# Graph layer on one core: the third expert layer in products of 512 columns, its tiles issued in two parts

## The reference, cut to what matters

```python
xn = layernorm(x)                                   # [3125, 256]
w = softmax(xn @ Wr + br)                           # [3125, 8], one gate per node and expert
h = relu(bn(einsum('fd,edh->feh', xn, W1) + b1))    # first layer
h = relu(bn(einsum('feh,ehk->fek', h, W2) + b2))    # second layer
y = einsum('feh,ehd->fed', h, Wo) + bo              # third layer
out = x + einsum('fed,fe->fd', y, w)                # gated sum over the experts
```

## Time and profile before

| what | value |
|---|---|
| three executions | 1117.34, 1115.76, 1119.72 us; median 1117.34 |
| profiled execution | 1118.59 us, its span 1116.6 us |
| PE busy | 945.6 us (85%), 5218 products |
| DVE busy | 749.9 us (67%), 1412 instructions |
| ACT busy | 586.4 us (53%) |
| third layer L1023 to L1025, products of 256 columns | 3 x 200 rows, 283 ns each |
| addition of outputs L1689 | 200 rows, 476 ns each |

### The profile page before, as it was taken

One profiled execution on the slowest core, in us unless ns is written; L12 is line 12 of the kernel. 1 busy time (PEld: TensorE's weight loads), 2 busy tenths in 40 slices (PEclk: granted clock), 3 DMA queues, 4 the chain that ended last, 5 costly groups with the idle time before them and its releaser, 6 DMA issues.

```text
span 1116.6 us, 15043 instructions
## 1 busy us (share of the span) xinstructions
PE 945.6 (85%) x5218; PEld 822.9 (74%) x5218; DVE 749.9 (67%) x1412; ACT 586.4 (53%) x1206; POOL 380.2 (34%) x408
## 2 busy tenths in 40 slices
PE   6868588887885889788863569999999999999997
PEld 5656477666774778666753458899998989898987
DVE  6748578767865787778785777787555655555554
ACT  4720155454553456364542336667756566666664
POOL 0236566666666666666667600000000000000000
PEclk9879799989987898888987769999999999999999
DMA  8414344344444344344436410020000000000012
GB/s 252 141 53 113 102 125 118 101 127 113 116 116 109 97 125 117 102 126 111 119 103 200 116 47 15 15 69 1 29 1 30 1 29 1 29 1 1 1 32 84
DMA packets 50362, 89.02 MB, mean 80 GB/s; under 512 B 9732, under 2 KB 33336, under 8 KB 50267
## 3 DMA queue, kind: packets, MB, share of 16 engines
q0 software_dynamic: 18768, 52.88, 17.5%
q1 hardware_dynamic: 30780, 34.66, 10.0%
q10 hardware_dynamic: 719, 0.27, 0.1%
HBM read 81.10 MB, written 6.68 MB: 79 GB/s over the span
## 4 chain that ended last, share of the span: by engine, by line
PE 51%; another core or an unknown queue 16%; ACT 15%; DVE 11%; issue 6%; DMA 0%; DVEq 0%; ACTq 0%
PE bank L1023 11%; PE bank L1025 11%; PE bank L1024 11%; PE bank L942 4%; PE bank L896 4%; ACT junk L579 2%; PE bank L817 2%; PE bank L852 2%; PE bank L949 1%; PE bank L931 1%; DVE oh L1360 1%; PE bank L810 1%; ACT TT L598 1%; ACT U L588 1%
## 5 line engine op out<-in xcount | busy, mean ns | idle before, releaser
L472 POOL DMA_INDIRECT G<-projected_rows,src_l x391 | 377.5, 965 | 260.9 <-issue 109.1
L721 ACT ACTIVATE hid<-bank,faff 128x512 f32<-128x512 f32 (+2 forms) x224 | 157.7, 723 | 115.5 <-PE bank L1025 113.7
L896 PE MATMUL bank<-G,oh 128*128 128x264 f32 x782 | 190.1, 402 | 18.9 <-DVE G L1383 10.8
L896 PEld LDWEIGHTS bank<-G,oh 128*128 128x128 f32 x782 | 154.7, 199 | 47.1 <-DVE G L1383 10.9
L1677 DVE TENSOR_TENSOR hil<-hid,hil 128x1024 fp32r<-128x1024 f32 (+2 forms) x56 | 61.0, 1089 | 101.2 <-ACT hil L729 101.2
L1383 DVE TENSOR_TENSOR G<-G,bank 128x3072 f32<-128x3072 f32 (+1 forms) x33 | 109.1, 3307 | 0.0
L604 ACT COPY feat_rows<-bank 128x256 f32<-128x256 f32 x25 | 9.3, 373 | 171.9 <-remote 163.1
L931 PE MATMUL bank<-feat_rows,wqkv 128*128 128x256 f32 (+1 forms) x312 | 75.3, 382 | 17.6 <-DVE baff L1484 11.4
L1023 PE MATMUL bank<-frh,ew 128*128 128x512 f32 (+3 forms) x228 | 84.9, 372 | 3.8 <-DVE frl L1652 3.8
L1689 DVE SCALAR_TENSOR_TENSOR feat_rows<-bank,gate,feat_rows 128x256 f32<-128x256 f32 (+1 forms) x200 | 83.2, 476 | 4.3 <-PE bank L1025 4.3
L1024 PE MATMUL bank<-frl,ew 128*128 128x512 f32 (+3 forms) x228 | 82.9, 364 | 0.0
(11 more groups left out here) (326 smaller groups left out, 2105.4 us busy)
## 6 DMA issues: line engine op xcount, KB each, us to landing
dstb<-targets SPq DMA_DIRECT2D x32, 384.0 KB, 5.1
G<-projected_rows,src_l POOLq DMA_INDIRECT x391
projected_rows<-sums SPq DMA_DIRECT2D x25, 132.0 KB, 2.2
x_in<-in_x SPq DMA_DIRECT2D x3, 1024.0 KB, 9.3
out<-feat_rows SPq DMA_DIRECT2D x23, 128.0 KB, 2.2
U<-in_x SPq DMA_DIRECT2D x4, 512.0 KB
TT<-in_W SPq DMA_DIRECT2D x8, 256.0 KB
wqkv<-in_W SPq DMA_DIRECT2D x8, 256.0 KB
```

The costliest lines, as they stand in the source:

```text
L472: g.indirect_dma_start(out=G[slot][:, c, :], out_offset=None, in_=table[:, :], in_offset=bass.IndirectOffsetOnAxis(ap=src_l[:, grp, c:c + ...
L721: A.activation(hid[layer][:, m, 0:cols], bank[2 * layer + m][:, 0:cols], ACT.Relu, bias=faff[:, 2 * layer + 1, j:j + 1], scale=faff[:, 2 * ...
L896: ins = T.matmul(b_seg[g % 2][:, 0:ROW], oh[g % 2][:, c, :], G[g % SLOTS][:, c, :], start=(c == 0), stop=(c == ch - 1))
```

## The change

The third layer's product of the high hidden values with both parts of the weights becomes one product of 512 columns (high weights and low weights side by side), in both halves k; the low hidden values by the high weights stay products of 256 columns. So a tile takes four products instead of six, and fills a whole bank with two sums of 256 columns. DVE adds both to `mixed`, with a wait between them. Every tile is a piece of its own: `third` signals `y_mm` per tile, `add_outputs` waits and signals per tile.

Since a tile takes a bank, the order changes. In steps below `WIDE` = 23, while banks 6 and 7 are in use, only banks 4 and 5 serve. PE issues tiles 0 and 1 behind the second layer of the next step, and tiles 2 and 3 (or 2) behind the first layer after that; DVE likewise. From step 23 on tile i has bank 4 + i, and all tiles are issued in one go. The shares are taken in seven groups of up to four tiles (`QUADS`), two tiles per bank, so that `WIDE` can begin at step 23, and DVE adds two tiles with one operation.

```diff
-PAIRS = [range(t, min(t + 2, NT)) for t in range(0, NT, 2)]
+QUADS = [[[t for t in (start + q, start + 4 + q) if t < NT] for q in range(2)]
+         for octet in range(0, NT, 8) for start in (octet, octet + 2) if start < NT]
...
+WIDE = SHARE + len(QUADS) + 1
...
+def pieces(n):
+    tiles = list(range(BLOCK_TILES[STEPS[n][1]]))
+    return [tiles[i:i + 1] for i in range(len(tiles))] if n >= 0 else [tiles[i:i + 2] for i in range(0, len(tiles), 2)]
+
+PIECES_TO = [0]
+for step in range(len(STEPS)):
+    PIECES_TO.append(PIECES_TO[-1] + len(pieces(step)))
...
-        def outputs_of(b):
-
-            for j in range(-(-columns(b) // P)):
-                size = min(P, columns(b) - j * P)
-                yield j, slice(j * P, j * P + size), bank[4 + j // 2][0:size, (j % 2) * F:(j % 2 + 1) * F]
+        def output_of(n, i, j):
+
+            size = min(P, columns(STEPS[n][1]) - j * P)
+            y = bank[4 + (i if n >= WIDE else i % 2)][0:size, 0:2 * F]
+            return slice(j * P, j * P + size), y
...
-            def third(n):
+            def third(n, chosen):
...
-                need(pe, s["y_add"], n)
-                for j, nodes_, y in outputs_of(b):
-                    for k in range(KC):
-                        ins = split_product(y, hidh[1][par][:, k, nodes_], hidl[1][par][:, k, nodes_], ew[:, e % 2, 0, 2, k, :], ew[:, e % 2, 1, 2, k, :], k)
-                ins.then_inc(s["y_mm"], 1)
+                if n == WIDE:
+                    pe.wait_ge(s["x2b"], SHARE_SUMS[-1])
+                for i in chosen:
+                    tiles = pieces(n)[i]
+                    if n < WIDE:
+                        need(pe, s["y_add"], PIECES_TO[n] + max(i - 1, 0))
+                    else:
+                        need(pe, s["y_add"], PIECES_TO[n - 1] + (min(i + 1, len(pieces(n - 1))) if n > WIDE else len(pieces(n - 1))))
+                    for j in tiles:
+                        nodes_, y = output_of(n, i, j)
+                        w = ew[:, e % 2, :, 2, :, :]
+                        lh, ll = hidh[1][par], hidl[1][par]
+                        high = y.rearrange("p (q f) -> p q f", q=2)
+                        T.matmul(high, lh[:, 0, nodes_], w[:, :, 0, :], start=True, stop=False)
+                        T.matmul(y[:, 0:F], ll[:, 0, nodes_], w[:, 0, 0, :], start=False, stop=False)
+                        T.matmul(y[:, 0:F], ll[:, 1, nodes_], w[:, 0, 1, :], start=False, stop=False)
+                        ins = T.matmul(high, lh[:, 1, nodes_], w[:, :, 1, :], start=False, stop=True)
+                    ins.then_inc(s["y_mm"], 1)
...
+                if 2 <= n < WIDE + 2 and len(pieces(n - 2)) > 2:
+                    third(n - 2, range(2, len(pieces(n - 2))))
                 second(n)
...
-                    third(n - 1)
+                    third(n - 1, range(2) if n - 1 < WIDE else range(len(pieces(n - 1))))
...
-            def add_outputs(n):
+            def add_outputs(n, chosen):
...
-                dve.wait_ge(s["y_mm"], n + 1)
-                need(dve, s["y_add"], n)
-                for j, nodes_, y in outputs_of(b):
...
+                need(dve, s["y_add"], PIECES_TO[n] + chosen[0] if len(chosen) else 0)
+                for i in chosen:
+                    tiles = pieces(n)[i]
+                    dve.wait_ge(s["y_mm"], PIECES_TO[n] + i + 1)
+                    for j in tiles:
...
+                        high, low_ = (y[:, q * F:(q + 1) * F].rearrange("p (c n) -> p c n", c=KC) for q in range(2))
+                        link(V.scalar_tensor_tensor(out=m, in0=high, scalar=gate[0:rows, t, e:e + 1], in1=m, op0=ALU.mult, op1=ALU.add))
+                        ins = V.scalar_tensor_tensor(out=m, in0=low_, scalar=gate[0:rows, t, e:e + 1], in1=m, op0=ALU.mult, op1=ALU.add)
+                    ins.then_inc(s["y_tile"] if n == len(STEPS) - 1 else s["y_add"], 1)
...
+            def add_shares(i, added):
+                quad = QUADS[i - 1]
+                dve.wait_ge(s["y_add"], added)
+                dve.wait_ge(s["bo_mm"], SHARE_TILES[i])
+                for q, tiles in enumerate(quad):
+                    m = mixed[:, tiles[0]:tiles[-1] + 1:STRIPS]
+                    V.tensor_tensor(m, m, bank[6 + q][:, 0:len(tiles) * F].rearrange("p (t c n) -> p t c n", c=KC, n=P), ALU.add).then_inc(s["x2b"], 1)
...
+                if 2 <= n < WIDE + 2 and len(pieces(n - 2)) > 2:
+                    add_outputs(n - 2, range(2, len(pieces(n - 2))))
                 if odd and b + 2 < BLOCKS:
                     statistics(b + 3)
...
-                    add_outputs(n - 1)
+                    add_outputs(n - 1, range(2) if n - 1 < WIDE else range(len(pieces(n - 1))))
```

More of the change, by code:

```diff
@@ L1 @@
+import itertools
 import math
@@ L78 @@
 NA = 16
-PAIRS = [range(t, min(t + 2, NT)) for t in range(0, NT, 2)]
+QUADS = [[[t for t in (start + q, start + 4 + q) if t < NT] for q in range(2)]
+         for octet in range(0, NT, 8) for start in (octet, octet + 2) if start < NT]
+QUADS = [[tiles for tiles in quad if tiles] for quad in QUADS]
+SHARE_SUMS, SHARE_TILES = [0], [0]
+for quad in QUADS:
+    SHARE_SUMS.append(SHARE_SUMS[-1] + len(quad))
+    SHARE_TILES.append(SHARE_TILES[-1] + sum(map(len, quad)))
+WIDE = SHARE + len(QUADS) + 1
 PIECES = HALVES[0] + list(zip(FIRST_TILE[1:], BLOCK_TILES[1:]))
@@ L432, in _ @@
             for b in range(BLOCKS - 1):
-                sp.wait_ge(s["y_add"], full + b + 1)
+                sp.wait_ge(s["y_add"], PIECES_TO[full + b + 1])
                 for t in tiles_of(b):
@@ L615, in split_weights @@
             def split_weights(e, m):
-                ends = ("h1_mm", KC), ("h2_mm", KC), ("y_mm", 1)
                 act.wait_ge(w_raw[e % 2], 48 * (e // 2 + 1))
@@ L620, in split_weights @@
                 else:
-                    act.wait_ge(s[ends[m][0]], ends[m][1] * (LAST_STEP[e - 2] + 1))
+                    done = LAST_STEP[e - 2] + 1
+                    signal, count = (("h1_mm", KC * done), ("h2_mm", KC * done), ("y_mm", PIECES_TO[done]))[m]
+                    act.wait_ge(s[signal], count)
                 A.copy(ew[:, e % 2, 0, m], raw[e % 2][:, m]).then_inc(s["w_hi"], 1)
@@ L726, in hidden @@
                 else:
-                    need(act, s["y_mm"], n - 1)
+                    need(act, s["y_mm"], PIECES_TO[max(n - 1, 0)])
                 act.wait_ge(done, n * KC + KC)
@@ L1088, in shares @@
                     pe.wait_ge(s["gt_ready"], 1)
-                for t in PAIRS[i - 1]:
-                    need(pe, s["x2b"], t - 1)
+                need(pe, s["x2b"], SHARE_SUMS[i - 1])
+                for part, q in itertools.product(range(2), range(2)):
+                    tiles = (QUADS[i - 1] + [[]])[q]
+                    if part >= len(tiles):
+                        continue
+                    t = tiles[part]
                     row = t % STRIPS * STRIP
-                    T.matmul(bank[6 + t % 2][:, 0:F], gT3[row:row + STRIP, t // STRIPS * P:(t // STRIPS + 1) * P],
+                    T.matmul(bank[6 + q][:, part * F:(part + 1) * F], gT3[row:row + STRIP, t // STRIPS * P:(t // STRIPS + 1) * P],
                              bo_split[row:row + STRIP, :], start=True, stop=True).then_inc(s["bo_mm"], 1)
@@ L1114, in _ @@
                 if n >= 1:
-                    third(n - 1)
+                    third(n - 1, range(2) if n - 1 < WIDE else range(len(pieces(n - 1))))
                 if n == SHARE:
                     gates_turned()
-                if SHARE < n <= SHARE + len(PAIRS):
+                if SHARE < n <= SHARE + len(QUADS):
                     shares(n - SHARE)
-            third(total - 1)
+            third(total - 1, range(len(pieces(total - 1))))
         @block.vector
@@ L1701, in split_gates @@
                 V.scalar_tensor_tensor(out=bo_split, in0=bo_raw, scalar=low[:, 0:1], in1=bo_hi, op0=ALU.mult, op1=ALU.add).then_inc(s["g3_in"], 1)
[L1703 to L1708 removed]
+            def add_shares(i, added):
[5 more added lines that the diff above has]
+                    V.tensor_tensor(m, m, bank[6 + q][:, 0:len(tiles) * F].rearrange("p (t c n) -> p t c n", c=KC, n=P), ALU.add).then_inc(s["x2b"], 1)
+                dve.wait_ge(s["x2b"], SHARE_SUMS[i])
             def rest_rows_of(b):
@@ L1759, in _ @@
                     split_gates()
-                if SHARE < n <= SHARE + len(PAIRS):
-                    add_shares(n - SHARE)
-            add_outputs(total - 1)
+                if SHARE < n <= SHARE + len(QUADS):
+                    add_shares(n - SHARE, PIECES_TO[n - 1] + 2)
+            add_outputs(total - 1, range(len(pieces(total - 1))))
 def _layout(i):
```

19 lines of the change are left out of this document (4 added, 15 removed).

## The result

The change makes the kernel slower: 1159.24 us median of four (1155.99 to 1160.63) against 1118.22 of four of the kernel before, a ratio of 1.0374 with an interval of 1.0358 to 1.0389. That is 41.0 us more; forecast were 37.2 more, 1154.5, in a range of 1141 to 1168.

What follows compares the result with a forecast made beforehand. PE was taken to bound the kernel, so any PE wait for DVE is lost in full. Terms 6.4 + 4.7 + 13.9 + 1.4 + 13.7 - 1.6 - 2.7 + 0.4 + 1 = +37.2 on 1117.3 gave 1154.5 us, range 1141 to 1168.

Steps and rivals of the forecast that it cites:

- The wide products: Third layer: a tile takes 0.691 us instead of 0.708, 0.017 less; -2.7 us over 156 tiles from step 12 on.
- The stalls of steps 13 to 24: PE waits for adds queued behind remainders on in-order DVE, 5.31 us against 4.11 of PE work; twelve stalls, +13.7 us.
- The interleaved steps: Steps 2 to 10: DVE's extra adds lengthen the loop; +4.7 us from R2 to R4, +13.9 from R4 to R10.
- R2: Start of step 2's second remainder (R(n) likewise for step n); forecast 709.6 instead of 703.19, +6.4 us.
- The clock: Start: new PE gaps, between 2.6 and 8.1 us, may lower the clock; charged +1 us, bounds 0 and 10.
- of which DVE's loop hides part: Start: a low clock for 5 us costs about 2.5 of PE time, partly hidden by DVE's loop; +1 us taken.
- The small edits: Shares of the output bias in 7 groups instead of 13, -1.6 us; the last two steps' adds, +0.4.
- B: Rival: only DVE's throughput counts, its idle time takes most of the extra work; about 1120 us, chance 0.04.
- D: Rival: the late steps wait too, 32 steps at 1 us more; about 1187 us, chance 0.03.
- E: Rival: faster, the stall in steps 13 to 24 vanishes as the second add costs nothing; about 1113 us, chance 0.03.
- C: Rival: the clock drops in the gaps of several steps, 5 us a stretch; about 1167 us, chance 0.07.
- F: Rival: the product with the two-piece operand is slow; +3 us, inside the forecast, no chance of its own.

Runs made afterwards that it cites:

- e1: The change, but DVE adds tiles 2 and 3 of a step ahead of the next first layer's remainder: 1147.21 us, ratio 1.0234 to the kernel before.
- e4: As e3, but in steps 0 to 22 tiles 2 and 3 are placed as in the change, still one add a tile: 1129.92 us, ratio 1.0075.
- e5: Kernel before in steps 0 to 13, the change's new order in 14 to 22, wide from 23, seven share groups: 1122.67 us against 1115.47.
- e2: The change, but in steps 0 to 22 DVE adds only each tile's high half, one operation: 1139.79 us, ratio 1.0171 to the kernel before.
- e7: The change with useless products in the start's two long PE gaps (20 and 16 of 512 columns): 1153.22 us against 1115.47 before.
- e6: The kernel before in all steps, with only the shares in seven groups of four tiles: 1113.96 us against 1115.47, ratio 0.9983.
- e3: Steps 0 to 22 as in the kernel before, 23 to 55 wide and shares as in the change: 1116.68 us against 1121.40, ratio 0.9960.
- e8: The change, but tiles 0 and 1 of a narrow step wait only for their own bank's add: 1152.27 us against 1115.47, ratio 1.0328.
- e9: The change with the edits of e1 and e8 together, on another chip: 1050.36 us against 1022.66 for the kernel before, ratio 1.0248.

## Why the prediction was right, point by point

**What bounds the kernel** was read rightly. PE had no slack, so its waits for DVE showed in the time, and the late steps stayed bound by PE: DVE's 76 us of work per 100 in them did not matter.

**The wide products** gave what the rows said. In step 48 four products make a tile, and tiles begin 0.70 us apart:

```profile
1043.92 0.40 PE L1105 MATMUL bank<-ew,even 128*128 128x512 f32 x1
1044.15 0.28 PE L1106 MATMUL bank<-ew,even 128*128 128x256 f32 x1
1044.27 0.28 PE L1107 MATMUL bank<-ew,even 128*128 128x256 f32 x1
1044.39 0.40 PE L1108 MATMUL bank<-ew,even 128*128 128x512 f32 x1
1044.62 0.40 PE L1105 MATMUL bank<-ew,even 128*128 128x512 f32 x1
```

From R30 to R53 the changed kernel gains 1.5 us on the one before over 83 tiles, 0.018 a tile, where the sum has 0.017. The two-piece operand costs nothing that can be seen. The estimate by the Trainium skill's fixed part (TensorE: Matmul & The Clock Gate, Back-to-back issue gap), a third of that, was too low here; the measurement decides.

**The stalls of steps 13 to 24.** The stage grew by 14.6 us, and e1, which takes only the order away, gives back 10.9 of them. The pattern was right as well: forecast were stalls of 2.0, 1.0, 1.0, 1.2, 0.6, 1.25, 0.9, 2.0, 1.0, 1.0 and 1.2, and the steps R14 to R24 are longer by 2.2, 1.4, 1.0, 1.3, 0.9, 1.2, 1.2, 2.2, 1.5, 1.1 and 0.8. The step that says why, "tile 0 for *all* adds of the step before", "behind the remainder", is shown by e1, e4 and e5, and its size by e5. They are undersized by 2.2 us: up to R24 the sum has eleven stalls, 13.2, less 0.7 for the wide products. About 0.9 of that is in the restarts: a product behind a wait has a row of 0.47 instead of 0.40, and the next one starts 0.31 behind it (857.94 and 858.25) instead of 0.23. Where the other 1.3 lies is open.

**The interleaved steps** came out at 5.4 and 13.6 for 4.7 and 13.9. Here the chain was right turn by turn, and not only in total: behind R4 the three periods were put at 23.6, 22.3 and 20.8 and are 23.5, 22.1 and 20.8. Of the 19.0 us that R2 to R10 grows, 8.3 go with the second addition (e2: 83.5 us instead of 91.8; before 72.8), 3.5 come between e4 (80.0) and e2, and 7.2 with the placement, part of it a low clock behind e4's gap.

**The clock** is the term that was mis-sized: it was charged with 1 and cost 2.5. "The new gaps lie between" was the open point. Gaps of 4.7 and 6.4 us did bring it down to its lower level (1.2 GHz), twice for some 7 us (a mean of 0.66 over 10 us is 6.8 us at half, 0.76 and 0.90 are 4.8 and 2.0 us). The first products behind them last 0.77 instead of 0.47 us:

```profile
694.25 0.77 PE L1105 MATMUL bank<-ew,even 128*128 128x512 f32 x1 [4.72 <-DVE feat_rows L1733]
...
707.85 0.76 PE L1105 MATMUL bank<-ew,odd 128*128 128x512 f32 x1 [6.44 <-DVE feat_rows L1733]
```

The step that failed is "of which DVE's loop hides part". In the time of this execution, 2.6 us earlier, the sum's chain has A(0) tile 2 at 694.3, which is what the row shows, the end of S(2) at 698.6 and R2 at 707.0. S(2) ended at 700.4 and R2 came at 708.81: 1.8 us late at both, so nothing was hidden. The second spell cost 0.6 more. DVE had to wait for PE's scores, which the chain of the sum doesn't have, and tile 0 of the next third layer, its tile 2 and R4 are each 0.6 to 0.7 later than R2 and the sum's distances give:

```profile
715.98 0.23 DVE L1698 TENSOR_REDUCE gate<-bank 128x32 f32<-128x64 f32 x1 [0.60 <-PE bank L1039]
```

e7 bears it out from the other side: with the gaps filled R2 is at 26.0, 6.5 over the kernel before, where the chain without the clock gives 6.4, and R4 another 24.9 later, where the sum has 24.8. "The clock stays at 1.00 but for the gaps of the start" did not hold either, with the two low spells around 768 and 792 us; they show in no milestone of the change, as R10 and R13 come when the sum has them.

**The small edits.** The shares' 1.6 was too small rather than too large: 1.9 by e6's times, with an interval from 0.6 to 3.1, and 2.4 by its milestones. The end's 0.4 wasn't there: from R53 to the end both take 19.2 us.

**The waits' total** was announced as 45 us in 35 waits and is 36 in 27. The time is lost all the same (R24 comes 43.5 later); the list counts them from the end of the last product's row, not from where the next could be issued.

**The rivals.** B fell by e1 and e2, D by e3, E by the result. C holds in part, 2.5 us of 41, at the start only. F fell by the row distances.

**The sum** gave 37.2 where the expert layers grew by 39.8 and the medians by 41.0. The clock was 1.5 short and the stalls 2.2, and the shares and the end took back about 1.2: so close a total is in part luck, while the two loops that make up most of it were read rightly.

## What to carry to other kernels

Before an operation is put behind another in the order of an in-order engine, add up the chain from what it stands behind to the engine that waits for it, and set it against what that engine has to do meanwhile. Here 5.3 us against 4.1 cost 1.2 in a step of 512 columns, and moving two lines on DVE gave most of that back in steps 13 to 24 (10.9 of 14.6 us), though not in the steps before, where DVE's own work and the banks close the loop. A saving of 17 ns a tile is worth having only where its price, a second addition and a bank a tile, falls on engines and banks with slack: in the late steps it was a gain, in the early ones a loss more than ten times as large.

## What had not been expected of the hardware

- The clock fell in gaps of 4.7 and 6.4 us of PE, of which the expert layers before had none longer than 2.6, and filling the gaps with useless products made the kernel 2 to 4 us faster. The gap of 2.6 us is no safe one: the clock stayed at 1.00 behind it in the kernel before and in e3, and fell behind the same gap in e5 and e6, where R4 came 1.6 us later.
- Beside e1 to e4 the kernel before took 1121 us, beside e5 to e8 1115 and beside e9, on another chip, 1022.66. The difference lies ahead of the expert layers: their first second-layer remainder starts at 587.8 us in e9 instead of 681.1, with the gathers' 391 instructions as long as ever (946 ns). Between 100 and 560 us of the changed kernel ACT's longest wait is for something outside the engines, and in e9 it is not among the waits listed:

```profile
ACT feat_rows L623 <- remote: 148.2, 20, 10.1
```

  Why is open; it wasn't tried.
